# A four-layer transformer kernel: layer 0 as one block with a four-pass weight quantizer, and three expert routings woven into their norms

## The reference

```python
# layer 0, attention
kv = ctx @ W_k.T + b_k;  out = p @ kv;  sim = out @ kv.T * 512**-0.5
sim = (sim - mean) * rsqrt(var + 1e-6) * gamma + beta;  x += softmax(sim)
# layer 0, feed-forward: weights are quantized in groups of 64, in bf16
scale = clip(mean(abs(w_g)), 1e-8);  q = clip(round(w_g / scale), -1, 1)
w = w + ((q * scale) - w)
# layers 1, 2, 3, feed-forward: a router (4, 8, 8 experts; top 2, 2, 4)
logits = x @ router;  top-k;  softmax over the chosen
```

## Time and profile before

| | |
|---|---|
| median of 3 runs | 3703.59 us (3701.0 to 3709.85) |
| the profiled execution | 3709.56 us, span 3707.7 us |
| busy: PE, DVE, ACT, POOL | 3084.9, 2243.4, 1801.0, 559.7 us |
| mean granted clock of TensorE | 0.908 of full speed |
| HBM traffic | 123 GB/s over the span |

### The profile page before, as it was taken

How to read it: one execution, slowest core, us unless ns; L and a number is a source line. 1 busy time by engine, 2 the same in 40 slices (tenths; PEclk the granted TensorE clock), 3 DMA queues, 4 the chain that set the end, 5 groups by cost and what they waited for, 6 DMA issues and landing times. The chain is left out here.

```text
span 3707.7 us, 55886 instructions
## 1 busy us (share of the span) xinstructions
PE 3084.9 (83%) x15750; PEld 2116.6 (57%) x15750; DVE 2243.4 (61%) x3802; ACT 1801.0 (49%) x3122; POOL 559.7 (15%) x1150
## 2 busy tenths in 40 slices
PE   3329999879872799928998699899898899979998
PEld 2117777645461688823333388788786333338886
DVE  6974445456443333358998444566556899936655
ACT  5643333535430455525777533566533577753443
POOL 2430000024422000040111040122111011100000
PEclk7659999879985899967999799999999799979999
DMA  4424444866361433343321262576643432102333
GB/s 139 143 96 136 136 137 136 306 166 149 90 233 40 127 107 108 104 149 95 80 62 36 77 209 93 176 244 235 214 139 95 127 79 62 42 21 91 94 98 113
DMA packets 241080, 461.87 MB, mean 125 GB/s; under 512 B 57444, under 2 KB 73956, under 8 KB 240402
## 3 DMA queue, kind: packets, MB, share of 16 engines
q1 hardware_dynamic: 207602, 343.64, 30.5%
q0 software_dynamic: 22480, 96.23, 7.7%
q10 hardware_dynamic: 10864, 20.45, 1.5%
HBM read 343.78 MB, written 113.77 MB: 123 GB/s over the span
## 5 line engine op out<-in xcount | busy, mean ns | idle before, releaser
L1702 DVE TENSOR_REDUCE at_maxima<-psum 128x1 f32<-128x512 f32 (+1 forms) x768 | 620.4, 859 | 36.0 <-PE psum L1610 30.2
L1683 ACT ACTIVATE at_probs<-psum 128x512 f32<-128x512 f32 x1024 | 528.6, 604 | 208.2 <-PE psum L1626 208.2
L1626 PE MATMUL psum<-at_qT,at_kT 50*128 50x512 f32 x1024 | 375.6, 456 | 71.0 <-ACT at_probs L1683 54.3
L601 PE MATMUL psum<-f_xT_hi,ffn_w_hi 128*128 x1024 | 406.5, 397 | 10.4 <-DVE f_xT_lo L313 2.8
L601 PE MATMUL psum<-f_xT_lo,ffn_w_hi 128*128 x1024 | 406.0, 397 | 0.0
L1610 PE MATMUL psum<-at_kT,at_qT 48*128 48x512 f32 x1024 | 387.0, 482 | 12.1 <-DVE at_maxima L1702 9.7
L1626 PEld LDWEIGHTS psum<-at_qT,at_kT 50*128 50x128 f32 x1024 | 171.0, 190 | 364.3 <-ACT at_probs L1683 243.8
L1639 PE MATMUL psum<-at_probs,at_vals 128*32 128x512 f32 x2048 | 281.2, 622 | 0.0
L393 PE MATMUL psum<-ident,n_normed 128*128 128x128 f32 x512 | 102.6, 369 | 202.1 <-ACT n_normed L356 159.5
L618 PE MATMUL psum<-ffn_w_hi,ffn_hid_hi 128*128 128x512 f32 x768 | 269.2, 391 | 1.3 <-ACT ffn_hid_hi L667 1.3
L490 ACT ACTIVATE ffn_w_hi<-ffn_w_raw 128x512 fp32r<-128x512 f32 x262 | 161.7, 633 | 156.2 <-PE psum L623 101.1
(11 more groups left out here) (381 smaller groups left out, 6701.5 us busy)
## 6 DMA issues: line engine op xcount, KB each, us to landing
ffn_w_raw<-in_stream SPq DMA_DIRECT2D x262, 256.0 KB, 2.7
ffn_w_hi<-quantized SPq DMA_DIRECT2D x66, 512.0 KB, 3.6
ffn_w_hi<-quantized SPq DMA_DIRECT2D x65, 256.0 KB, 3.2
at_qT<-q_hi SPq DMA_DIRECT2D x256, 64.0 KB, 2.3
ffn2a_w_raw<-in_shared2a SPq DMA_DIRECT2D x26, 512.0 KB
qz_raw<-in_stream SPq DMA_DIRECT2D x17, 768.0 KB, 4.2
quantized<-qz_quant POOLq DMA_DIRECT2D x16, 768.0 KB, 3.5
gathered<-zeros SPq DMA_DIRECT2D x1, 12288.0 KB
```

The costliest lines, as they stand in the source:

```text
L601: mm = pe.matmul(hid_ps[h][s][0:n, :], wt[s][:, w], xt[:, c, bass.ds(b * S, S)], start=(c == 0 and i == 0), stop=(c == DC - 1 and i == len ...
L1626: pe.matmul(scoreT[turn_of(n)][:, :], kT[r][half(h % 2, USED + 2), t * P:(t + 1) * P], qT[r][half(h % 2, USED + 2), h // 2, :], start=True ...
L1683: act.activation(probs[n % RING][:, :], scoreT[turn_of(n)][:, :], ACT.Exp, scale=factor).then_inc(exped, 1)
L1702: dve.tensor_reduce(maxima[g % 2][:, h:h + banks, t], scores, AX.X, ALU.max).then_inc(maxed, 1)
```

## The change

Four things, in one diff.

1. `Quantizer`: no `limit`; VectorE does six instructions instead of four (two tensor_scalar, four tensor_tensor). SP's and TensorE's waits count two ScalarE results a chunk instead of three, and TensorE waits for the magnitude only.
2. `stage_xattn0`: `scaled`, `logits` and the exponentials stay in the PSUM banks of sim; loops over batches are written out, so that work for a fifth batch falls away; TensorE's sim matmul of the next batch waits for `x_made`. `repeat` is issued by SP after the load of chunk 5 and not waited for there.
3. n0, xattn0, n1 and ffn0 are one block. TensorE's transposes of n1 wait until all updates of x are made (`banks_free`), VectorE's measuring for its batch, and SP waits for all stores and the repeat ahead of the first weight load (`stream_made`).
4. `weave_route` gives the norms of layers 1, 2, 3 a hand-written order that takes in the router products, with two column banks instead of one (banks 4, 5, and 6 for the turned ones); `weigh` is the ranking, as before. In layers 2 and 3 `start()` is written after the woven part and ahead of `weigh()`.

```diff
@@ class Quantizer
-        act.wait_ge(self.split, 6 + 3 * c + 1)
-        act.activation(self.limit[s][:, :], self.mag[s][:, :], ACT.Copy, scale=1.0 / self.OVER_HALF).then_inc(self.split, 1)
...
     def quantize(self, dve, c, s):
         dve.wait_ge(self.scaled, c + 2)
-        dve.scalar_tensor_tensor(out=self.over[:, :], in0=scale, scalar=self.LEAST, in1=self.limit[s][:, :],
-                                 op0=ALU.max, op1=ALU.is_lt).then_inc(step, 1)
-        dve.wait_ge(step, 3 * c + 1)
-        dve.scalar_tensor_tensor(out=self.what[:, :], in0=scale, scalar=self.LEAST, in1=self.over[:, :],
-                                 op0=ALU.max, op1=ALU.mult).then_inc(step, 1)
-        dve.wait_ge(step, 3 * c + 2)
-        dve.tensor_tensor(self.what[:, :], self.what[:, :], mag, ALU.subtract).then_inc(step, 1)
-        dve.wait_ge(step, 3 * c + 3)
+        if c > 0:
+            dve.wait_ge(self.worked, c)
+        dve.tensor_scalar(over, scale, self.LEAST, 0.5, ALU.max, ALU.mult).then_inc(step, 1)
+        dve.tensor_scalar(what, scale, self.LEAST, 1.0, ALU.max, ALU.mult).then_inc(step, 1)
+        dve.wait_ge(step, 5 * c + 1)
+        dve.tensor_tensor(over, over, mag, ALU.is_lt).then_inc(step, 1)
+        dve.wait_ge(step, 5 * c + 2)
+        dve.tensor_tensor(what, what, mag, ALU.subtract).then_inc(step, 1)
+        dve.wait_ge(step, 5 * c + 4)
+        dve.tensor_tensor(what, what, mag, ALU.add).then_inc(step, 1)
+        dve.wait_ge(step, 5 * c + 5)
         dve.wait_ge(self.done, c + 1)
-        dve.tensor_tensor(self.result[s][:, :], mag, self.what[:, :], ALU.add).then_inc(self.worked, 1)
+        dve.tensor_tensor(self.result[s][:, :], what, over, ALU.mult).then_inc(self.worked, 1)
@@ stage_xattn0
-                pe.wait_ge(scaled_made, TB * b + t + 1)
+                pe.wait_ge(x_made, TB * b + t + 1)
...
-                act.activation(probs[t][:, :], logits[:, t, :], ACT.Exp, bias=minus_max[:, t:t + 1],
+                act.activation(sim[t][:, :], sim[t][:, :], ACT.Exp, bias=minus_max[:, t:t + 1],
...
-                dve.scalar_tensor_tensor(out=logits[:, t, :], in0=scaled[:, t, :], scalar=rstd[:, t:t + 1], in1=beta[:, :],
+                dve.scalar_tensor_tensor(out=sim[t][:, :], in0=sim[t][:, :], scalar=rstd[:, t:t + 1], in1=beta[:, :],
...
-                dve.scalar_tensor_tensor(out=xt, in0=probs[t][:, :], scalar=inv[:, t:t + 1], in1=xt,
+                dve.scalar_tensor_tensor(out=xt, in0=sim[t][:, :], scalar=inv[:, t:t + 1], in1=xt,
@@ weave_route, the orders (waits left out)
+        # TensorE
+            turn(0)
+            turn(1)
+            pe.wait_ge(w_lo_made, 1)
+            columns_of(0)
+            turn(2)
+            turn_columns(0)
+            columns_of(1)
+            turn(3)
+            for b in range(1, B):
+                turn_columns(b)
+                if b + 1 < B:
+                    columns_of(b + 1)
+        # ScalarE
+            apply(0)
+            act.activation(w_hi[:, :, :], raw[:, :, :], ACT.Copy).then_inc(w_hi_made, 1)
+            apply(1)
+            move(0)
+            apply(2)
+            move(1)
+            copy_columns(0)
+            apply(3)
+            move(2)
+            copy_columns(1)
+            move(3)
+            copy_columns(2)
+            copy_columns(3)
+        # VectorE
+            measure(0)
+            aggregate(0)
+            measure(1)
+            make_shift(0)
+            aggregate(1)
+            dve.wait_ge(w_hi_made, 1)
+            dve.tensor_tensor(w_lo[:, :, :], raw[:, :, :], w_hi[:, :, :].bitcast(F32), ALU.subtract).then_inc(w_lo_made, 1)
+            measure(2)
+            make_shift(1)
+            aggregate(2)
+            split(0)
+            measure(3)
+            make_shift(2)
+            aggregate(3)
+            split(1)
+            make_shift(3)
+            take(0)
+            split(2)
+            take(1)
+            split(3)
+            take(2)
+            take(3)
@@ build_program
-                made, buffers, _ = stage_norm(k, "n0", xT=xT, joined=room)
-                stage_xattn0(k, xT, dram["stream0"], scratch["quantized"], room, made, buffers)
-        with ExitStack() as ctx:
-            xT = transposed(ctx, "f0")
-            with stage_room(k) as room:
-                made, buffers, _ = stage_norm(k, "n1", xT=xT, joined=room)
+                made, normed, _ = stage_norm(k, "n0", xT=xT, joined=room)
+                x_made, x_before, stream_made = stage_xattn0(k, xT, dram["stream0"], scratch["quantized"], room, made)
+                made, buffers, _ = stage_norm(k, "n1", xT=xT, joined=room, normed=normed, banks_free=(x_made, x_before + NT),
+                                              before=lambda dve, b: dve.wait_ge(x_made, x_before + TB * b + TB))
                 stage_ffn(k, "ffn0", xT, scratch["quantized"], ACT.Silu, True, 1, [P] * 16, 2, exact=True, rms=True, joined=room,
-                          xT_made=made, buffers=buffers)
+                          xT_made=made, buffers=buffers, stream_made=stream_made)
```

More of the change, by code:

```diff
@@ L220, in await_store, with repeat, stage_norm @@
         pool.sem_inc(self.left, 1)
[L222 to L229, removed]
+    def repeat(self, sp, chunks):
+        sp.wait_ge(self.left, 4)
+        sp.dma_start(self.w_out[chunks:chunks + 2], self.w_out[0:2]).then_inc(self.repeated, DMA)
+def stage_norm(k, nm, xT=None, tokens=None, rows=None, joined=None, beside=None, before=None, bank=0, woven=None, banks_free=None, normed=None):
     with stage_room(k, joined) as room:
@@ L480, in _ @@
                 sp.sem_inc(sem, CR)
+            for made in stream_made:
+                sp.wait_ge(*made)
             load_w1(sp, 0, 0, 0)
@@ L795, in _ @@
         quantizer.load(sp, 0, 0)
[L796 to L799, removed]
+        for c in range(1, chunks):
+            quantizer.load(sp, c, c % 2)
+            if c == PER + 1:
+                quantizer.repeat(sp, chunks)
     @block.tensor
@@ L807, in keys @@
             pe.wait_ge(outT_made, b + 1)
[L808 removed]
+            pe.matmul(kvT_ps, wkT[:, :], ctxT[:, b * S:(b + 1) * S], start=True, stop=True).then_inc(kvT_product, 1)
             pe.wait_ge(kvT_made, b + 1)
@@ L815, in _ @@
         pe.wait_ge(*xT_made)
-        with pe.Fori(0, B) as b:
+        for b in range(B):
             pe.wait_ge(kv_hi_made, b + 1)
@@ L848, in _ @@
         keys(0)
-        with act.Fori(0, B) as b:
+        for b in range(B):
             def take_apart(i):
@@ L882, in _ @@
         keys(0)
-        with dve.Fori(0, B) as b:
+        for b in range(B):
             quantizer.quantize(dve, PER * b, 0)
@@ L893, in _ @@
                 dve.wait_ge(aggregated, TB * b + t + 1)
-                dve.scalar_tensor_tensor(out=scaled[:, t, :], in0=sim[t][:, :], scalar=moments[:, t, 0:1], in1=gamma[:, :],
+                dve.scalar_tensor_tensor(out=sim[t][:, :], in0=sim[t][:, :], scalar=moments[:, t, 0:1], in1=gamma[:, :],
                                          op0=ALU.subtract, op1=ALU.mult).then_inc(scaled_made, 1)
@@ L920, in _ @@
         quantizer.start_store(pool)
-        with pool.Fori(0, B) as b:
+        for b in range(B):
             quantizer.store(pool, PER * b, 0)
@@ new lines, in weave_route @@
+    ctx, block = room.memory, room.block
+    raw, w_hi, w_lo = k.sb(ctx, f"{nm}_raw", [P, DC, R]), k.sb(ctx, f"{nm}_w_hi", [P, DC, R], F32R), k.sb(ctx, f"{nm}_w_lo", [P, DC, R], F32R)
+    columns = k.sb(ctx, f"{nm}_columns", [P, S])
+    logits = k.sb(ctx, f"{nm}_logits", [P, NT, R])
+    beats = k.sb(ctx, f"{nm}_beats", [P, E, NT, E])
+    rank = choice if choice is not None else k.sb(ctx, f"{nm}_rank", [P, NT, E])
+    shifted, exps, chosen, kept = (k.sb(ctx, f"{nm}_{n}", [P, NT, E]) for n in ("shifted", "exps", "chosen", "kept"))
@@ new lines, in weave_route @@
+    top1, total, inv = (k.sb(ctx, f"{nm}_{n}", [P, NT]) for n in ("top1", "total", "inv"))
+    columns_ps, turned_ps = [room.banks[4 + s][0:R, :] for s in range(2)], room.tiles(6)
+    zeroed, landed, w_hi_made, w_lo_made, product, columns_made, turned, taken, compared, step, exped = k.sems(
+        ctx, nm, "zeroed landed w_hi_made w_lo_made product columns_made turned taken compared step exped")
+    if bias is not None:
+        bias_row = k.sb(ctx, f"{nm}_bias", [P, E])
+        bias_landed, = k.sems(ctx, nm, "bias_landed")
@@ new lines, in dve, with take @@
+        def dve(dve, measure, aggregate, make_shift, split):
+            def take(b):
+                dve.wait_ge(turned, b + 1)
+                dve.tensor_copy(logits[:, b * TB:(b + 1) * TB, :], turned_ps[:, :, 0:R]).then_inc(taken, 1)
+            measure(0)
[20 more added lines that the diff above has]
+            take(3)
@@ L1976, in _ @@
         def _(dve):
-            with dve.Fori(0, B) as b:
-                dve.wait_ge(turned, b + 2)
-                dve.tensor_copy(logits[:, bass.ds(b * TB, TB), :], turned_ps[:, :, 0:R]).then_inc(taken, 1)
-            dve.wait_ge(taken, B + 1)
```

(1 more changed line is left out.)

163 lines of the change are left out of this document (74 added, 89 removed).

## The result

The changed kernel takes 3650.5 us (median of four executions, 3645.7 to 3665.3), the kernel before in the same set 3706.7 (3701.0 to 3720.9). The ratio is 0.986, 95% interval 0.984 to 0.988. The profiled execution of the changed kernel took 3651.9 us with a span of 3650.2, against 3709.6 and 3707.7: the span is 57.5 us shorter, where the sum of the prediction came to 45.8. By medians the gain is 56.2 us.

The account below looks back on a forecast made before the run. VectorE's own list was taken to bound the first stage, and chains of waits the norms and routings. 17.0 + 11.2 - 1.0 + 1.4 + 0.7 + 13.9 + 2.6 = 45.8 us off 3703.59 gave 3657.8, range 3642 to 3681.

Parts of the forecast that it names:

- (a): First stage: logits and probabilities stay in PSUM, so two VectorE lines stop waiting for GpSimd's multiply; 17.0 us gained.
- R5: Rival, first stage: PSUM output with one SBUF input still excludes GpSimd, so 17 us are lost; 3675, chance 0.05.
- (b): First stage's quantizer: six shorter VectorE instructions a chunk, no limit pass; 11.2 - 1.0 + 1.4 us gained.
- R1: Rival, quantizer: tensor_scalar runs at tensor_tensor's rate, 0.96 us, so 12.8 us less gain; 3670.6, chance 0.11.
- R4: Rival, quantizer: four passes take 1.75 us each, a chunk 3.5 us longer than before; slower, 3724, chance 0.03.
- the -1.0: Quantizer at batch ends: the shorter first pass waits for nearly all of GpSimd's 3.1 us multiply; 1.0 us lost.
- (c): One block from first stage to next norm: VectorE goes straight on, 14.9 less 1.0 for late rstd; 13.9 us gained.
- The keys of a fifth batch: First stage: VectorE's work on keys for a fifth batch falls away; 0.7 us gained.
- (d): Woven routings of layers 1 to 3: 2.5, -0.5 and +0.6 us, 2.6 gained, bounds -20 and +8.
- the chain: Layer 1's woven routing, step by step through its waits: last copy 45.4 us after the first measurement, before 48.6.
- R2: Rival, woven routings: hand order leaves TensorE in bursts at 1.2 GHz, 22 us less gain; 3680, chance 0.09.
- R3: Rival, woven routings: the weave hides products well, 9 us in each routing instead of 0.9; 3634, chance 0.05.

Follow-up runs that it names:

- experiment 4: experiment 1's kernel with scaled, logits and probabilities in SBUF again; median 3696.5 us, 12.3 above experiment 1, ratio 0.994.
- experiment 3: experiment 1's kernel with the old quantizer and ScalarE's limit pass back; median 3697.9 us against 3684.2 for experiment 1, ratio 0.994.
- experiment 1: The changed kernel with layer 0's first stage and its second norm in two blocks again, late repeat; ratio 0.989 to the kernel before.
- experiment 5: The changed kernel with the routings of layers 1 to 3 behind their norms again; ratio 0.987, the three stretches 4.6, 0.8 and 2.3 us longer.
- experiment 7: The changed kernel with another hand order in the weave on ScalarE, VectorE and TensorE; ratio 0.980, three stretches 28.5 us shorter than experiment 6.
- experiments 1 to 10: The changed kernel rerun, parts undone, or other hand orders, on two chips where the kernel before takes longer than in the first set.
- experiments 11 and 12: experiment 10's kernel with layer 2's row sends paced, or only half sent; 740.3 and 739.6 us from ranking to next norm, on another chip.
- experiment 6: The changed kernel unaltered, run once more on the same chip as experiment 7; ratio 0.984, median 3665.1 us.
- experiment 10: The changed kernel with experiment 7's weave order and each quantizing placed between PSUM work; ratio 0.977, 3637.6 us.
- experiment 11: experiment 10's kernel with each of layer 2's 32 row-sending DMAs waiting until the one before landed; ratio 0.975, 3613.6 us.

## Why the prediction came out as it did

The forecast of 3657.8 us against 3650.5 is off by 7.3, and the mechanisms are those it named. The gain was missed by more: 45.8 forecast, 56.2 by medians. 3.1 us of that don't show in the 7.3 only because the kernel before came out at 3706.7 in this set instead of 3703.6. The sizes were these.

- (a) 17.0: measured 18.0, all in the two lines (experiment 4). The choice of 0 for a PSUM output holds: 750 and 751 ns, against medians of 744 and 752 without it, and the maxima take 691 ns from PSUM and 686 from SBUF (experiment 4). R5 is refuted. The Trainium skill, VectorE: DVE Perf Modes, section The TRN2 errata, has 120 fixed cycles for a PSUM source and 58 for SBUF; by that, an estimated 65 ns would come on top of each. The trace doesn't agree: the three differences are 6, -1 and 5 ns.
- (b) 11.2 - 1.0 + 1.4 = 11.6: measured 14.1 (experiment 3; 12.6 in the chunks, 1.5 at the start). The new chunk of 4.75 was right (4.74), with tensor_scalar at 0.55 for 0.56, so R1 and R4 are refuted. Two steps were mis-sized. The old chunk lasts 5.53 from start to end where its four durations give 5.4, so the gain is 0.79 a chunk and not 0.7 (unrounded the forecast's own durations give 0.67, 10.7 us in all). And the -1.0 wasn't there: the wait behind a batch's end cost 2.85 us before (a chunk of 8.38) and costs 2.93 now.
- (c) 13.9: measured 13.7 (experiment 1), the late power included (-1.0 forecast, -0.8 measured).
- The keys of a fifth batch: between the kernels the stage from first to last quantizing is 174.7 - 143.45 = 31.3 us shorter, and 18.0 + 12.6 leave 0.7, as forecast. That is a remainder and no measurement: the 18.0 was taken beside the new quantizer, where an update waits longer, and with the 17.0 that the two lines had before it would be 1.7. Unrolling and the second load were taken at 0; the first quantizing comes 1.1 us earlier beyond the 1.5 of `limit`, less than this stretch scatters.
- (d) 2.6: measured 7.7 (experiment 5). This is the term that was most wrong. The applies came 5.5, 11.9, 21.0 and 27.7 us after the start, as the chain had them (12, 21, 28), and the last logits were done at 43.9 instead of 45.4: the turned columns behind turn(3) were done at 35.6, not 36.6, and each of the last two rounds took 4.1 us, not 4.3. The stretch before is 48.9 to the ranking, not 48.6, and 0.7 of the 3.2 us that the chain gave was written off for the clock with no row for it. In layers 2 and 3 +0.8 and +2.3 were measured where -0.5 and +0.6 were forecast. R2 (the clock stays at 1.2 GHz) didn't come: the granted clock of the three stretches is 0.75 to 0.81, before 0.70 to 0.78. R3's size, 9 us in each routing, doesn't come with the order of the change; another hand order passes it (experiment 7: 14.1, 10.6 and 11.7 us shorter than before). And where layer 2 has the slow stretch, 6 to 8 of the 7.7 us are taken back behind the ranking (experiment 5); in the first set they were not (739.4 us there, 742.3 before).

So 18.0 + 14.1 + 13.7 + 0.7 + 1.1 + 7.7 = 55.3 of the 57.5 us; the other 2.2 are the balance of stages that weren't touched. They scatter by more than that between the two traces: from the first routing's ranking to the second's start the changed kernel is 9.1 us slower, and from layer 1's first norm to its second 6.6 faster, with the same code.

## What to carry to other kernels

Where two engines exclude each other on SBUF, put work that reads PSUM beside the other engine's long instruction, and compare its length with that instruction's: 0.3 and 0.5 us too short was paid in each of four batches. A weave is as good as its hand order: no engine's list should stand at a wait for which another batch's ready work could pass; the same instructions took 134 us in one order and 106 in another. And where the whole time scatters by more than a term is worth, measure the term between two fixed points of the trace, and find out first how well these repeat: here within 0.5 us in some stretches, while another scattered by 1.9. Then look for what the stages behind give back: of the 28.5 us of experiment 7, 10.4 stood in the medians.

## What the runs showed of the hardware that was not expected

In layer 2 GpSimd sends rows by 32 indirect DMAs beside the shared feed-forward. In all ten traces of experiments 1 to 10, taken on two chips, TensorE's products issue slowly from 40 to 50 us behind the ranking on; in the traces of the first set, and of experiments 11 and 12, they don't. By stretch, the changed kernel in the first set:

```profile
2112.90:2117.90 5.00, 5.00 (x23) 4.05 (x23) 2.01 (x3) 2.71 (x4) 4.09 (x4) 1.00 0.93 371
2117.90:2122.90 5.00, 5.00 (x24) 4.09 (x23) 1.19 (x2) 0.32 (x1) 3.78 (x5) 1.00 0.79 231
```

and the same kernel in experiment 6, at the same distance (45 to 55 us behind the ranking):

```profile
2120.00:2125.00 5.00, 1.63 (x5) 1.03 (x5) 2.60 (x3) 2.17 (x3) 3.78 (x5) 0.87 0.47 178
2125.00:2130.00 5.00, 3.28 (x6) 1.69 (x6) 0.01 (x1) 0.00 (x0) 3.78 (x5) 0.50 0.86 280
```

Five or six products in 5 us instead of 23, and the granted clock falls to 0.50 behind it. Between ranking and the next norm it costs 19.6 us (758.9 against 739.4), more than any single term of the change, and it ends about when the last of the 32 is issued, some 60 us behind the ranking. What it costs differs with the order of the work ahead of it, in one or two traces each: 8.6 us with the old routings (750.9 in experiment 5, 742.3 in the kernel before), 25 with the order of experiment 7 (765.2 in experiment 10, 740.3 in experiment 11). The kernel before is 14 to 17 us slower on the two chips where this was seen, so it probably meets it there as well, but no trace of it was taken there. Why TensorE is slow stays open: the trace shows no semaphore that it waits for.
